# Cutting the output products of each chunk into smaller parts that begin at the next chunk's first slot

## What is computed

```python
xn = _layernorm(x, ln_g, ln_b)
xn = xn * (1.0 + scale[:, None, :]) + shift[:, None, :]
...
def step(h, inp):
    dt_t, B_t, C_t, u_t = inp
    dA = jnp.exp(dt_t[:, :, None] * A)
    h = h * dA + (dt_t * u_t)[:, :, None] * B_t[:, None, :]
    y = jnp.einsum('bdn,bn->bd', h, C_t)
...
y = y * jax.nn.silu(z)
return jnp.einsum('bsd,ed->bse', y, out_proj_w)      # out_proj_w: 512 x 1024
...
return x + gate[:, None, :] * x_ssm
```

## Time and profile before

| | |
|---|---|
| three runs, median (range) | 2281.68 us (2277.33 to 2285.43) |
| the profiled execution, span | 2280.4 us |
| own time of the profiled execution | not given beside its span; it lies among the three runs' times |
| PE, DVE, ACT, POOL busy | 90%, 88%, 75%, 77% of the span |
| first layer's slots (first scan to last) | 66.3 to 1789.2 us |
| beginning of chunks 1 to 7 (first scan) | 289.5, 505.2, 719.4, 933.1, 1147.0, 1366.5, 1578.9 us |

### The profile page before, as it was taken

How to read it: one execution, slowest core, us unless ns; L and a number is a source line. 1 busy time by engine, 2 the same in 40 slices (tenths; PEclk the granted TensorE clock), 3 DMA queues, 4 the chain that set the end, 5 groups by cost and what they waited for, 6 DMA issues and landing times. The chain is left out here.

```text
span 2280.4 us, 30708 instructions
## 1 busy us (share of the span) xinstructions
PE 2057.2 (90%) x10240; PEld 1328.4 (58%) x10240; DVE 2013.0 (88%) x2226; ACT 1705.3 (75%) x3154; POOL 1763.7 (77%) x1012
## 2 busy tenths in 40 slices
PE   8888989889998998899979898998977899999999
PEld 3354555455555555555545455545554688888878
DVE  4899999999999999999989999999999766666666
ACT  4688788888897889788877888897667355566655
POOL 0587799999999999999999999999999422132225
PEclk9899999999999999999999999999988999999999
DMA  7612331251125122522332242225001210111113
GB/s 236 248 45 72 98 144 51 70 179 63 57 69 181 56 70 60 190 88 66 96 141 61 70 142 95 54 68 184 33 28 54 95 34 28 41 56 61 40 56 129
DMA packets 95098, 205.94 MB, mean 90 GB/s; under 512 B 10141, under 2 KB 13469, under 8 KB 94942
## 3 DMA queue, kind: packets, MB, share of 16 engines
q1 hardware_dynamic: 94942, 203.99, 27.9%
HBM read 171.91 MB, written 17.30 MB: 83 GB/s over the span
## 5 line engine op out<-in xcount | busy, mean ns | idle before, releaser
L1464 POOL TENSOR_TENSOR arena<-arena 128x1024 f32<-128x1024 f32 x512 | 1198.1, 2363 | 131.8 <-ACT arena L630 125.6
L1060 DVE TENSOR_TENSOR_SCAN arena<-ps,arena 128x512 f32<-128x512 f32 x1024 | 1234.2, 1247 | 31.1 <-ACT ps L630 19.7
L630 ACT ACTIVATE ps<-arena 128x512 f32<-128x512 f32 x1087 | 715.2, 676 | 247.9 <-DVE arena L1060 123.0
L343 PE MATMUL ps<-keep,arena 128*128 128x128 f32 x4096 | 544.8, 283 | 113.0 <-POOL arena L1464 102.5
L343 PEld LDWEIGHTS ps<-keep,arena 128*128 128x128 f32 x4096 | 478.3, 146 | 288.2 <-POOL arena L1464 167.0
L281 PE MATMUL ps<-arena 128*128 128x512 f32 x1024 | 465.4, 600 | 19.1 <-issue 18.3
L1045 DVE TENSOR_TENSOR arena<-ps,arena 128x1024 f32<-128x1024 f32 x379 | 453.5, 1196 | 20.3 <-PE ps L343 16.4
L281 PEld LDWEIGHTS ps<-arena 128*128 128x128 f32 x1024 | 188.8, 192 | 239.1 <-issue 238.5
L1433 POOL TENSOR_TENSOR arena<-arena 128x1024 f32<-128x1024 f32 x133 | 314.3, 2363 | 9.7 <-PE ps L343 9.6
L630 ACT ACTIVATE arena<-ps 128x512 f32<-128x512 f32 (+2 forms) x386 | 205.9, 538 | 54.1 <-PE ps L281 23.5
L333 PE MATMUL ps<-arena 128*128 128x512 f32 x512 | 236.0, 601 | 4.7 <-DVE arena L1081 3.8
(11 more groups left out here) (150 smaller groups left out, 2636.7 us busy)
## 6 DMA issues: line engine op xcount, KB each, us to landing
arena<-scr_bc SPq DMA_DIRECT2D x128, 512.0 KB, 8.6
arena<-in_inT SPq DMA_DIRECT2D x184, 256.0 KB, 2.8
arena<-arena SPq DMA_DIRECT2D x112, 128.5 KB, 2.3
arena<-in_x SPq DMA_DIRECT2D x17, 512.0 KB, 3.9
scr_x<-arena SPq DMA_DIRECT2D x32, 256.0 KB, 2.0
arena_b<-scr_x SPq DMA_DIRECT2D x16, 512.0 KB, 3.7
arena_c<-scr_x SPq DMA_DIRECT2D x32, 256.0 KB, 2.9
out<-arena_c SPq DMA_DIRECT2D x32, 256.0 KB, 2.0
```

Source lines behind the costliest of these rows:

```text
L343: last = e.matmul(YP[:, 128 * q:128 * q + 128], hb[G % R][:, i, 128 * q:128 * q + 128], ident, start=(g == 0 and i == 0 and q == 0), stop= ...
L630: return e.activation(o_, i_, f, **kw)
L1060: e.tensor_tensor_scan(H, DA[s % 4], H, h0, MUL, ADD).then_inc(v_sc)
L1464: e.tensor_tensor(H, H, Ct[:, GN * g:GN * g + GN, :], MUL).then_inc(g_w)
```

## The change

The table OUTM now gives, for a slot, the first and the last (exclusive) of the products done in it. The four groups of eight are cut into 14 parts of one to three products (five in unit 0, three in unit 1, six in unit 2) instead of 8 parts of four. The evacuation of the first group goes from slot 13 to slot 14. The first part stands in slot (0, 0). The x rows of the groups n = 0 and 1 are fetched in slot (7, 5) of the chunk itself, no longer in slot (0, 2) of the next. (For chunk 7, whose products stand in a tail of their own, nothing changes.)

```diff
-        OUTM = {(0, 4): 0, (0, 11): 4, (1, 1): 8, (1, 5): 12, (2, 2): 16, (2, 7): 20, (2, 9): 24, (2, 12): 28}
-        OUTA = {(0, 13): 0, (1, 10): 1, (2, 9): 2, (3, 2): 3}
+        OUTM = {(0, 0): (0, 2), (0, 2): (2, 4), (0, 6): (4, 6), (0, 8): (6, 7), (0, 12): (7, 8),
+                (1, 1): (8, 11), (1, 2): (11, 13), (1, 6): (13, 16),
+                (2, 2): (16, 19), (2, 4): (19, 21), (2, 6): (21, 24), (2, 10): (24, 27), (2, 12): (27, 30), (2, 14): (30, 32)}
+        OUTA = {(0, 14): 0, (1, 10): 1, (2, 9): 2, (3, 2): 3}
...
                     if c > 0 and (j, pr) in OUTM:
-                        n, q0 = divmod(OUTM[j, pr], 8)
-                        if q0 == 0:
-                            e.wait_ge(g_gw, 4 if c < 5 else 8)
-                            out_P = bank(("out", c - 1, n), (a_x1, 4 * (c - 1) + n + 1), 128 * c + OUT_AT[n] + 0.6)
-
-                            e.wait_ge(d_xr[n % 2], 16 * ((4 * (c - 1) + n) // 2 + 1))
-                            e.matmul(out_P, ident, xr[n % 2], start=True, stop=False)
-                        for q in range(q0, q0 + 4):
+                        for k in range(*OUTM[j, pr]):
+                            n, q = divmod(k, 8)
+                            if q == 0:
+                                e.wait_ge(g_gw, 4 if c < 5 else 8)
+                                out_P = bank(("out", c - 1, n), (a_x1, 4 * (c - 1) + n + 1), 128 * c + OUT_AT[n] + 0.6)
+                                e.wait_ge(d_xr[n % 2], 16 * ((4 * (c - 1) + n) // 2 + 1))
+                                e.matmul(out_P, ident, xr[n % 2], start=True, stop=False)
                             out_mm(c - 1, n, q, out_P)
...
-                if c > 0 and (j, pr) == (0, 2):
-                    load_xr(4 * (c - 1))
-                    load_xr(4 * (c - 1) + 1)
+                if more and (j, pr) == (7, 5):
+                    load_xr(4 * c)
+                    load_xr(4 * c + 1)
```

## The result

| | before | changed |
|---|---|---|
| time, median of five runs (range) | 2284.69 us (2277.33 to 2286.31) | 2292.46 us (2290.53 to 2295.67) |
| ratio to before, 95% interval | | 1.0043 (1.0028 to 1.0058) |
| profiled execution, span | 2280.4 us | 2291.3 us (its own time: 2293.11 us) |

The account below looks back on a forecast made before the run. It took a relay of DVE and POOL as the bound, with DVE's waits for PE at chunk beginnings paid in full. -8.9 + 6 + 0 + 0 = -2.9 us gave 2279 us, range 2270 to 2290.

Parts of the forecast that it names:

- Rival 1: POOL sets the pace, so only a third of the 8.9 us passes: 2285 us; chance 0.17.
- (a): First group's products in slots (0, 0) and (0, 2), outside chunk 5: clock stays up, DVE's wait goes, 8.9 us gained.
- Rival 2: Clock falls at the chunk's beginning all the same, moved products delay nsums: 2297 us; chance 0.13 together with another rival.
- (b): Chunk 5's first group waits for the output weights with nsums queued behind it: 6 us lost, bounds 4.1 to 9.9.
- Rival 3: Chunk 5 loses nothing, another order of events takes up the delay: 2273 us; chance 0.25.
- (c): Second and third group, units 1 and 2: moves offset each other, 0; bounds 0.9 us either way in each of seven chunks.
- (d): x rows fetched in a quiet unit instead of among the loads of B and C: nobody waits for them, 0.

Follow-up runs that it names:

- E: Kernel before, with the first group in slots (0, 0), (0, 2), (0, 4), (0, 10), (0, 12) except in chunk 5, x rows fetched in unit 7: 2276.0 us, ratio 0.9961.
- C: Kernel before, with the new parts of the first group in chunk 5 alone and the x rows fetched in unit 7: 2290.2 us, ratio 1.0024.
- I: Changed kernel with second, third and fourth group as before the change, first group in its new parts in every chunk: 2286.3 us, ratio to before 1.0015.
- H: Changed kernel with the first group cut as in E, but old in chunk 5; new parts of units 1 and 2 kept: 2284.2 us, ratio to before 0.9999.
- D: Kernel before, with only the x rows moved, fetched in slot (7, 5): 2284.8 us, ratio 1.0003.

## Why the prediction was wrong

*What bounds the kernel.* Right. A wait of DVE at the chunk's beginning is paid in full; E took the waits away and reached 212.4 us in chunk 2, as chunk 6 had suggested, and C's chunk 6 lost the 2.0 us as soon as it had the wait. Rival 1 (POOL sets the pace) falls with E.

*(a), 8.9 us gained.* The step that failed is "What is late next is nothing on PE". I worked out PE's times up to the nsum of the pair (0, 1) and stopped there. The idle time after `dt_mm`, which arose because the block of slot (0, 4) no longer stood there, and `y_back` with three products in front of it were one and two steps further on. The clock fell again for 3.4 us, and the wait went from `expand` (1.92 us) to `y_fin` (1.58 us). Rival 2 had named the falling clock, but at another place and with another price. Of the 8.9 us, chunks 1 to 3 gave 0.3, 0.3 and 0.6 in unit 0 and chunks 4 and 7, where the clock held, their full 1.9 and 1.0; chunk 6 lost 1.7. That leaves 2.4. The parts of E, which keep the idle time filled, give 8.7 in the same units.

*(b), 6 us lost in chunk 5.* Right in mechanism, in every link of the chain: from the end of the nsum at 1170.91 to the end of the exponential at 1175.45 it was 4.54 us (4.55 in the working). Mis-sized was the time at 1.2 GHz, 6.1 us after PE's restart instead of 4.2, so that unit 0 lost 6.8 us (39.9 against 33.1). Another 2 us came in later units, where the clock fell again for 3.4 us at a time (at 1198.4 in unit 1 and 1276.9 in unit 4) and where the later groups' new parts stand too. Together 8.9, inside the bounds of 4.1 to 9.9. C, with the first group alone, lost 6.0 in unit 0, the forecast, and 7.2 in the chunk; there the clock was low for 4.4 us after the restart, nearly the 4.2 of the working. Rival 3 (no loss) did not come about.

*(c), 0.* Wrong: some 6 us, from I (1.0015) against the changed kernel (1.0043), and 8 us in the presence of the gain (H against E). I set off the parts of unit 2 against each other within that unit, and did not ask what the two products of slot (2, 14) push back. PE is busy for 25.03 of 26.1 us in unit 3 of E, so there they are not hidden. In the profile of the changed kernel unit 2 is shorter by 3.3 us over the seven chunks, as the working has it, but unit 3 is longer by 5.6 and unit 1 by 1.5. It was also wrong to leave the bounds of 0.9 us in each of seven chunks out of the range.

*(d), 0.* Right (D: 1.0003).

*The sum.* In the profiled executions 10.9 us: 8.9 in chunk 5, 2.0 in chunk 6 and 0 over the rest, where 6 was forecast for chunk 5 and -8.9 for the others. By units it is 4.4 in the seven units 0, where -2.9 was forecast, and 5.3 in the other units of chunks 1 to 7, where 0 was; the rest, 1.2, lies outside of them. Had only (b) been mis-sized, by the whole 2.9, the time would have been that of before; that the kernel became slower takes (a) and (c).

What stays open: how the 6.8 us of chunk 5's unit 0 divide between the wait and the clock. Worked out, three products at 2.4 GHz would have ended at 1161.60 + 2.7 = 1164.3, not at 1167.1, which makes 2.8 us of clock; no run held the clock up there with the wait in place. Three executions with this order of the first group point the same way: PE ran at 1.2 GHz for 4.4 us after its restart in C, 5.5 in I and 6.1 in the changed kernel, and unit 0 lost 6.0, 6.6 and 6.8 us. Carried on to no low clock at all, that leaves some 4 us for the wait, an estimate, near the lower bound of 4.1. With the old slots the length of the low clock cost nothing there: in H it was 17.1 us as well, and unit 0 took 33.1 us as before.

```profile
1149.60:1166.70 17.10, 10.80 (x30) 6.92 (x31) 10.55 (x10) 11.73 (x23) 17.10 (x9) 0.50 0.42 160
```

## What to carry to other kernels

When work is moved into one idle time of an engine whose granted clock falls after idle time, follow that engine to the next two waits: the work is missing where it stood, and a new idle time can open there. Over the first 15 us of chunk 2 PE was idle for 4.9 us in the changed kernel and 4.4 us in E, nearly the same; the clock fell in the one, whose longest stretch was 2.41 us, and not in the other, whose longest was 1.53 us. A group of products whose first member waits for something rare (here the weights of the second batch entry) must not stand in front of work that others wait for, even if it is harmless in six of seven cases. And each part that ends later than before needs its own cover: look at how full the engine is where it now stands.

## What the runs showed of the hardware that I had not expected

After an idle time of 2.41 us in chunk 2 of the changed kernel TensorE's clock fell to 1.2 GHz for 3.4 us, and after one of 2.39 us at the same place of the same order in I it stayed at 2.4 GHz. With the same order in unit 0, one execution can differ from another at a chunk's beginning by 1.6 to 2 us (28.3 and 26.7 us here, 26.6 and 28.6 us in chunk 6 of the kernel before and of C). How much of the 9 us between the kernel's own five runs this makes is not shown. A fall of 3.4 us in the middle of a chunk costs too: in unit 4 it came with 1.2 us more (28.1 to 28.7 us in place of 26.9 to 27.5), in chunk 4 before the change, chunk 6 of E and chunk 5 of C.

The low stretches were 3.4, 6.8, 10.2, 13.7 or 17.1 us long. How long the clock stays low once work has resumed did not follow the length of the idle time: it was 6.1 us after one of 9.99 us (changed kernel, chunk 5), 4.2 us after one of 5.72 us (before, chunk 5), and 9.2 us after one of 4.95 us (H, chunk 5).
